# Attention in nine tiles of 512 columns per round where there were twelve of mixed width, and the second transpose of the first expert stage one slot sooner

## The reference

```python
# causal attention: 16 heads of 64, all in float32
s = einsum('bhid,bhjd->bhij', q * scale, k)
gm = max(s, axis=-1)                       # over all keys, the masked ones too
p = where(causal_mask, 0.0, exp(s - gm))
out = einsum('bhij,bhjd->bhid', p, v) / (sum(p, -1) + EPS)
...
# experts: 32 of 128 x 128, the two best of each token
w_masked = zeros_like(rw).at[arange(T)[:, None], idx].set(vals)
acc = acc + x_flat * w_e[:, None] @ W_e    # for each expert
```

## Time and profile before

| | |
|---|---|
| median of 3 runs | 1938.06 us (1935.25 to 1942.48) |
| the profiled execution | 1936.94 us, span 1935.2 us |
| PE, matmul busy | 1785.5 us (92%) |
| DVE | 1447.8 us (75%) |
| POOL | 1309.6 us (68%) |
| ACT | 1007.9 us (52%) |
| granted TensorE clock, mean | 0.958 |

### The profile page before, as it was taken

How to read it: one execution, slowest core, us unless ns; L and a number is a source line. 1 busy time by engine, 2 the same in 40 slices (tenths; PEclk the granted TensorE clock), 3 DMA queues, 4 the chain that set the end, 5 groups by cost and what they waited for, 6 DMA issues and landing times. The chain is left out here.

```text
span 1935.2 us, 32851 instructions
## 1 busy us (share of the span) xinstructions
PE 1785.5 (92%) x11830; PEld 1301.3 (67%) x11830; DVE 1447.8 (75%) x2497; ACT 1007.9 (52%) x2066; POOL 1309.6 (68%) x1327
## 2 busy tenths in 40 slices
PE   6999999999999999999999999959998478849998
PEld 4767667676767776767766767648776355538886
DVE  6777777777777777777777777559888166778998
ACT  3444444444445454444444444447887555437776
POOL 1777667667776676676666766839888245617998
PEclk9999999999999999999999999979999588969999
DMA  3000000000000000000000000000000000000000
GB/s 89 2 1 1 1 1 1 1 1 1 1 2 1 1 1 1 1 1 1 1 1 2 1 1 1 23 22 1 1 1 1 7 1 1 1 0 7 12 12 17
DMA packets 15089, 10.89 MB, mean 6 GB/s; under 512 B 433, under 2 KB 14546, under 8 KB 14930
## 3 DMA queue, kind: packets, MB, share of 16 engines
q1 hardware_dynamic: 14930, 8.80, 1.6%
HBM read 6.70 MB, written 2.10 MB: 5 GB/s over the span
## 5 line engine op out<-in xcount | busy, mean ns | idle before, releaser
L1222 DVE TENSOR_REDUCE attn_neg<-attn_shared 128x2 f32<-128x1024 f32 x512 | 614.7, 1223 | 272.7 <-PE attn_shared L1355 268.8
L1105 ACT ACTIVATE attn_prob<-attn_shared 128x1024 f32<-128x1024 f32 (+3 forms) x384 | 311.2, 813 | 451.6 <-PE attn_shared L1383 350.9
L1017 POOL TENSOR_TENSOR attn_row_sum<-attn_row_sum,attn_prob 128x1024 f32<-128x1024 f32 (+3 forms) x256 | 417.2, 1630 | 129.7 <-ACT attn_prob L1105 110.0
L497 ACT ACTIVATE experts_weighed<-experts_y,kept_gate 128x128 f32<-128x128 f32 x1024 | 279.0, 404 | 68.2 <-PE experts_y L724 53.6
L1012 POOL TENSOR_TENSOR attn_row_sum<-attn_prob 128x1024 f32<-128x1024 f32 x64 | 135.4, 2116 | 217.7 <-ACT attn_prob L1105 215.2
L580 DVE SCALAR_TENSOR_TENSOR experts_acc<-experts_y,kept_gate,experts_acc 128x128 f32<-128x128 f32 x960 | 262.4, 340 | 20.9 <-PE experts_y L724 18.9
L1351 PE MATMUL attn_shared<-attn_qk_hi 64*128 64x512 f32 x1024 | 226.5, 425 | 11.4 <-DVE attn_qk_lo L1235 2.4
L1241 DVE RECIPROCAL attn_den<-attn_den 128x256 f32<-128x256 f32 x128 | 214.7, 1719 | 12.1 <-ACT attn_den L1129 12.1
L1355 PE MATMUL attn_shared<-attn_qk_hi,attn_qk_lo 64*128 64x512 f32 x1024 | 211.3, 392 | 0.0
L1353 PE MATMUL attn_shared<-attn_qk_lo,attn_qk_hi 64*128 64x512 f32 x1024 | 210.2, 390 | 0.0
L722 PE MATMUL experts_y<-kept_w_hi,kept_xT_hi 128*128 128x512 f32 x512 | 205.9, 402 | 0.1
(11 more groups left out here) (227 smaller groups left out, 3265.2 us busy)
## 6 DMA issues: line engine op xcount, KB each, us to landing
kept_x<-in_L_attn_a_x_dram SPq DMA_DIRECT2D x4, 512.0 KB, 9.3
out_dram<-kept_x SPq DMA_DIRECT2D x8, 256.0 KB, 2.3
attn_prob<-in_L_attn_a_Wkv_dram SPq DMA_DIRECT2D x2, 512.0 KB, 6.9
kept_half_raw<-_ffn_expert_weights_dram SPq DMA_DIRECT2D x2, 512.0 KB, 4.5
last_other_half<-_ffn_expert_weights_dram SPq DMA_DIRECT2D x2, 512.0 KB, 4.6
attn_prob<-in_L_attn_a_Wq_dram SPq DMA_DIRECT2D x1, 512.0 KB, 5.1
attn_wo<-in_L_attn_a_Wo_dram SPq DMA_DIRECT2D x1, 512.0 KB, 5.4
attn_bo<-in_L_attn_a_bo_dram SPq DMA_DIRECT2D x1, 64.0 KB, 5.5
```

The source lines that it names most:

```text
L497: ins = act.activation(weighed[n][:, e, :], y[fill(pair, quad, odd) % RING][:, e * D:(e + 1) * D], ACT.Copy, scale=k.gate[:, c, quad * PER ...
L1017: pool.tensor_tensor(row_sum[n][:, :, at:], row_sum[n][:, :, at:], src[:, :, at:], ALU.add).then_inc(add_ok, 1)
L1105: act.activation(prob[n % RING][:, :, at:], buffer((p, i))[:, :, at:], ACT.Exp).then_inc(exp_ok, 1)
L1222: dve.tensor_reduce(neg[p % 2][:, :, b, half], buffer((p, b, half))[:, :, :], AX.X, ALU.max, negate=True).then_inc(max_ok, 1)
```

## The change

The twelve parts of a round are kept, in another order, and grouped into nine tiles. A tile is two banks of PSUM, one per head, of 512 columns. The narrow parts share a tile by twos: 384 with 128 columns, 256 with 256, and 384 with 128. The exponential is one instruction of 512 columns per head for each tile. Masks, additions and products still go by part. The order of the row stages is now a string for each of the two, and the nine tiles of a round just fill the ring of nine. In the expert stage the second transpose comes 8 slots after the base in place of 9, and `high` and `low` stand first behind the weighing and the gated sums.

```diff
-    STATS, VARIANCE, ROOT, SCALE, NORMAL, TURN = (-7, 0), 1, 2, 3, ((4, 4), (5, 6)), (6, 9)
+    STATS, VARIANCE, ROOT, SCALE, NORMAL, TURN = (-7, 0), 1, 2, 3, ((4, 4), (5, 6)), (6, 8)
...
                     weigh(pair, turn)
+                    for half in range(2):
+                        if turn_at(slot, half) is not None:
+                            high(turn_at(slot, half), half)
...
                     quad_sums(pair, turn)
+                    for half in range(2):
+                        if turn_at(slot, half) is not None:
+                            low(turn_at(slot, half), half)
                     if turn == 2 and pair:
                         merge(pair - 1)
...
-    ST_UNITS = [(1, j) for j in (0, 1, 2, 5, 6, 7, 3, 4)] + [(0, j) for j in range(4)]
+    PARTS = [(1, j) for j in (0, 1, 2, 5, 7, 3, 4, 6)] + [(0, j) for j in range(4)]
+    TILES = [[(1, 0)], [(1, 1)], [(1, 2)], [(1, 5), (1, 7)], [(1, 3)], [(1, 4)], [(1, 6), (0, 2)], [(0, 0)], [(0, 1), (0, 3)]]
+    FIRST_TILES, FIRST_PARTS = 5, 6
+    HALF_TILES = 7
-    STAGE = "stststststssst"
-    UNITS = len(ST_UNITS)
+    STAGES = ("stststststsss", "stsstsstssts")
+    UNITS = len(PARTS)
...
+    def place_of(part):
+
+        at = 0 if part != TILES[tile_of(part)][0] else columns(part)
+        return slice(at, at + HALF - columns(part))
...
-            def exponential(p, i):
-                n = UNITS * p + i
-                at = columns(i)
-                old_p, old_i = divmod(n - RING, UNITS)
+            def exponential(p, t):
+                n = len(TILES) * p + t
+                old_p, old_t = divmod(n - RING, len(TILES))
                 act.wait_ge(shift_ok, n + 1)
                 if n >= RING:
-                    act.wait_ge(pv_ok, n - RING + 1)
-                    act.wait_ge(add_ok, ADDS * old_p + ADDED[old_i])
+                    last = max(PARTS.index(part) for part in TILES[old_t])
+                    act.wait_ge(pv_ok, UNITS * old_p + last + 1)
+                    act.wait_ge(add_ok, ADDS * old_p + ADDED[last])
...
-                act.activation(prob[n % RING][:, :, at:], buffer((p, i))[:, :, at:], ACT.Exp).then_inc(exp_ok, 1)
+                act.activation(prob[n % RING][:, :, :], buffer((p, t))[:, :, :], ACT.Exp).then_inc(exp_ok, 1)
...
+            def shifted(p, t):
+
                 hi, lo, neg_row = qk_hi[p % 2], qk_lo[p % 2], neg_rows
+                shared_free((p, t))
+                for part in TILES[t]:
+                    half, j = part
+                    if part in ((1, 0), (0, 2)):
+                        pe.wait_ge(rows_ok, 2 * p + 2 - half)
+                    keys = slice(j * P, (j + 1) * P)
+                    at = slice(half * HALF + columns(part), (half + 1) * HALF)
+                    out = buffer((p, t))[:, :, place_of(part)]
...
```

More of the change, by code:

```diff
@@ L816, in out_group, with columns, tile_of, tile_count @@
         return g if r % 2 and 0 <= g < ROUNDS // 2 else None
-    def columns(i):
-        half, j = ST_UNITS[i]
+    def columns(part):
+        half, j = part
         return max(0, (j - 4 * half) * P)
+    def place_of(part):
+        at = 0 if part != TILES[tile_of(part)][0] else columns(part)
+        return slice(at, at + HALF - columns(part))
+    def tile_of(part):
+        return next(n for n, tile in enumerate(TILES) if part in tile)
+    def tile_count(p, i):
+        return len(TILES) * p + tile_of(PARTS[i]) + 1
     def is_diagonal(i):
-        half, j = ST_UNITS[i]
+        half, j = PARTS[i]
         return j >= 4 * half
@@ L914, in halves_done, with slot @@
             return max(0, 2 * n - 1)
+        def slot(p, part):
+            return prob[(len(TILES) * p + tile_of(part)) % RING]
         def buffer(u):
@@ L989, in mask @@
             def mask(p, i):
-                at = columns(i)
-                diagonal = prob[(UNITS * p + i) % RING][:, :, at:at + P]
-                pool.wait_ge(exp_ok, UNITS * p + i + 1)
+                at = place_of(PARTS[i]).start
+                diagonal = slot(p, PARTS[i])[:, :, at:at + P]
+                pool.wait_ge(exp_ok, tile_count(p, i))
                 pool.tensor_tensor(diagonal, diagonal, below[:, :].unsqueeze(1).to_broadcast([P, 2, P]),
@@ L998, in add @@
             def add(p, i):
-                half, j = ST_UNITS[i]
+                half, j = PARTS[i]
                 n = 1 - half
-                at = columns(i)
-                src = prob[(UNITS * p + i) % RING]
+                at = columns(PARTS[i])
+                src = slot(p, PARTS[i])[:, :, place_of(PARTS[i])]
                 if i in (0, 8):
@@ L1048, in _ @@
                         normal(r - 1, 0)
-                    for p, i in turned_units(r, t):
+                    for p, i in parts(r, t):
                         if is_diagonal(i):
@@ L1364, in turned @@
                 ins.then_inc(turned_ok, 1)
-            def shifted(p, i):
-                half, j = ST_UNITS[i]
+            def shifted(p, t):
                 hi, lo, neg_row = qk_hi[p % 2], qk_lo[p % 2], neg_rows
[L1370 to L1383, removed]
+                shared_free((p, t))
+                for part in TILES[t]:
+                    half, j = part
+                    if part in ((1, 0), (0, 2)):
[3 more added lines that the diff above has]
+                    out = buffer((p, t))[:, :, place_of(part)]
+                    for h in range(2):
+                        pe.matmul(out[:, h, :], hi[head(h), 1, keys], hi[head(h), 0, at], start=True, stop=False)
+                    for h in range(2):
+                        pe.matmul(out[:, h, :], hi[head(h), 1, keys], lo[head(h), 0, at], start=False, stop=False)
+                    for h in range(2):
+                        pe.matmul(out[:, h, :], lo[head(h), 1, keys], hi[head(h), 0, at], start=False, stop=False)
+                    for h in range(2):
+                        ins = pe.matmul(out[:, h, :], pick[head(h), :], neg_row[head(h), at], start=False, stop=True)
@@ L1384, in shifted @@
                 ins.then_inc(shift_ok, 1)
             def product(p, i):
-                half, j = ST_UNITS[i]
-                g, first = p // 2, columns(i)
+                part = PARTS[i]
+                half, j = part
+                g, first = p // 2, columns(part)
                 if i == 0:
@@ L1396, in product @@
                 else:
-                    pe.wait_ge(exp_ok, UNITS * p + i + 1)
+                    pe.wait_ge(exp_ok, tile_count(p, i))
                 for h in range(2):
                     cols = slice((2 * (p % 2) + h) * DH, (2 * (p % 2) + h + 1) * DH)
-                    ins = pe.matmul(pv[head(h), first:], v[g % 2][:, j, cols], prob[(UNITS * p + i) % RING][:, h, first:],
+                    ins = pe.matmul(pv[head(h), first:], v[g % 2][:, j, cols], slot(p, part)[:, h, place_of(part)],
                                     start=(j == 0), stop=(i in (7, 11)))
```

33 lines of the change are left out of this document (14 added, 19 removed).

## The result

The changed kernel takes 1913.87 us, the median of 4 runs (1912.57 to 1914.20), against 1936.92 for the kernel before in the same comparison. A fourth run of the kernel before, 1935.79 us, moved its median from 1938.06. The ratio is 0.9875, with a 95% interval of 0.9854 to 0.9896: faster, by 23 us between the medians and 24 by the ratio, 1.2% and clear of the noise. In a second comparison it was 0.9878 (0.9865 to 0.9892).

What follows compares the result with a forecast made beforehand. PE was taken to bound attention, losing time to PSUM waits, and to stall at routing in the expert stage. 18.9 + 7.0 - 0.5 = 25.4 us off the 1938.06 median gave 1912.7 us, range 1896 to 1930.

Steps and rivals of the forecast that it cites:

- PE bounds attention, and its loss is holes in the row stages: Attention: PE sets the pace; holes are waits for PSUM, and unit order can give at most 1.12 us a round.
- The first row stage, 0.07 gained: First row stage of a round: no unit held, margin only 0.1 us, 10.65 us for 10.72.
- The second row stage, 10.24 laid out: Second row stage: one hold of 0.4 us plus 0.08 restart, 10.24 us for 10.78, 0.54 gained.
- Behind the second stage: After the second row stage: the next waits for DVE, which also ends 0.57 us earlier, so PE's gain is kept.
- Sum of attention, 18.9 less 0.5: Attention: 0.61 us in each of 31 rounds, 18.9 us, less 0.5 once for GpSimd's additions in the last round.
- Fewer exponentials count for nothing: Attention, ScalarE: nine exponentials for twelve save 0.5 us a round, worth nothing as ACT has 19 us idle.
- The experts, 7.0: Expert stage: an earlier transpose removes two routing stalls, 8.4 us, partly taken back; 7.0 taken, bounds 8.4 and 2.
- The rival without holds: Attention: DVE's lead carries over the "s s t" pattern, so no holds; 43 us gained in all, 1895 us; chance 0.12.
- the holes only move: Row stages: thin margins become waits that eat the attention gain, only the experts' gain stays, 1931 us; chance 0.09.
- The routing does not stall: Expert stage; the rival judged said the routing stalls as before, by the clock or another transpose, 1920 us; chance 0.12.
- The lockstep rival: Second row stage runs in lockstep with DVE, takes 12.54 us, and the kernel is slower at 1983 us; chance 0.03.
- The rule of the Trainium skill: PE in row stages: short rests while cycling PSUM banks swing the clock between two levels, so more to gain.

Runs made afterwards that it cites:

- e7: Changed kernel with the second row stage ordered s t s t s t s t s s s s (s scores, t turned): 1907.1 us, ratio 0.9833.
- e9: Changed kernel with the second-stage order of e7 and one of VectorE's two second-stage reciprocals moved behind the low parts: 1906.3 us, ratio 0.9840.
- e10: Changed kernel with only one of VectorE's two second-stage reciprocals moved behind the low parts: 1914.6 us, ratio 0.9879.
- e1: Kernel before with the expert part alone: second transpose 8 slots after the base, high and low moved up in their queues: 1930.2 us, ratio 0.9957.
- e4: Kernel before with only high and low moved to the front of their queues, transposes left in slots 28, 44 and 60: 1935.7 us, ratio 0.9984.
- e8: Changed kernel with two exponentials for each packed tile, one per part, tiles and order as changed: 1914.9 us, ratio 0.9874.
- e3: Kernel before with only the second transpose 8 slots after the base, high and low still last in their queues: 1927.4 us, ratio 0.9944.
- e5: Changed kernel in the same order, but each part in its own tile, twelve tiles and a ring of ten: 1983.2 us, ratio 1.0228.

## Why the prediction was right, point by point

It said 1912.7 us in a range of 1896 to 1930, and 1913.87 was measured.

- **PE bounds attention, and its loss is holes in the row stages**: right. PE's work stayed the same, the holes shrank, and the time of a round followed.
- **The first row stage, 0.07 gained**: none was. Two terms were misread and cancel. The packed tile of 384 and 128 was costed at 1.22 and takes 1.10 (615.00 to 616.10), because 0.12 of the 0.52 read for the 128 part belongs to what follows a stage, not to the part. Now the last score unit bears it, with 0.83 (619.23 to 620.06) for the 0.70 put down. What is missing is at the last unit, where the margin of 0.1 us was indeed too thin: the unit ahead of it takes 0.77, a hold with its restart.
- **The second row stage, 10.24 laid out**: 10.28. The hold at the fifth score unit was put at 0.4 and a restart of 0.08, and it is 0.35 and 0.07. The rest of the agreement is partly luck: the packed tile takes 1.09 for 1.22 (637.14 to 638.23), and the last unit 0.87 for 0.70 (638.23 to 639.10).
- **Behind the second stage**: the forecast that nothing is taken back was right, with a rest of 7.36 us for 7.38. The reason given was wrong. That step said that the next row stage waits for the low parts of VectorE. It does not (e7, e9, e10), and so the layout of e7 could be passed over.
- **Sum of attention, 18.9 less 0.5**: 16.3 less 1.3. A round gained 0.52 for 0.61. The 0.5 for the last round was right: GpSimd makes the product wait there, and it starts its first addition without a rest, where it had rested 1.13 us, because it comes out of the round before with more work left. The other 0.8 is the clock in the last output product, 0.61 for 0.70, of which the sum had nothing. What sets that clock was not tested, but it is not the change alone: with attention as before the product takes 5.1 us in e1 and 5.9 in e4.
- **Fewer exponentials count for nothing**: right (e8).
- **The experts, 7.0**: 7.1 in the profiles (7.3 from first to last fill) and 7.5 alone (e1). The price of a stall, a wait and a fall of the clock behind it, held: the same fills, counted across the two stalls, come 4.1 and 4.3 us sooner, together the 8.4 of the sum. What was taken back held in size only. The 1.2 us put down for ScalarE are not in the trace, where the longest delay of a fill between the transposes of slots 27 and 43 and their routings is 0.24 us. Instead 0.4 us are lost at the start of the stage, where the clock is low for longer (the 31st fill comes 11.82 us after the first for 11.44), and 0.7 in slots 50 to 58, which no run explains. But the place in the queues, on which the prediction counted too, added nothing (e3).
- **Not foreseen**: 2.2 us of the profiled gain come from the two lengths of the linear stage and are no part of the change. So the closeness of the forecast is partly luck: without them the profiled gain is 22.2 us for the 25.4 of the sum. That the forecast started from a median of 1938.06, and not 1936.92, brought it another 1.1 us nearer to the time measured.
- **The rivals.** The rival without holds did not come, as two maxima in a row did cost PE 0.35 us. That the holes only move did not come either: where units of 512 columns alternate, they follow one another after 0.92 and 0.70. The routing does not stall, 0.29 us behind the last fill, with `low` 0.06 us ahead of it. The lockstep rival did not come; what does run slower than before is the unpacked order of e5.
- **The rule of the Trainium skill** (TensorE: Matmul & The Clock Gate, "A second HAM failure mode: psum-queue depth-cycling") was set against the row and did not hold here. The granted clock is 1.00 through the rounds of the kernel before, with holes of 0.3 us in each row stage, and removing holes gave their own length and no more. The page tells it of another kernel, in bf16, and gives no length of the rests.

Of the versions tried, e7 beats the kernel before by 31 us and the changed one by 7. It differs from the change in one string. e9 is as fast and has more edits.

## What to carry to other kernels

When an engine reads as busy all the time, read the starts of its units and compare each kind of unit with its own shortest distance: the sum of the excess is what an order can give. A narrow tile in a ring of PSUM buffers takes a whole buffer, so try to pack narrow parts by twos (here 1914 us for 1983), and try more than one order of the units, since the layout by hand found the large holes here and not the best order (e7, 7 us less). Before a chain of waits is taken to bound a stage, look in the code at which of its steps the first unit waits for.

## What the runs showed of the hardware

- After a rest of PE of 2.52 or 2.54 us the matmuls of 512 columns came every 0.43 us for a while. After rests of 1.96 and 1.95 us in one run (e4) they came every 0.23 us the first time and every 0.43 the second. So a rest of 1.96 us costs about 2 us or about 3.6, an estimate that adds 1.6 for the lower clock.
- The linear stage, in which PE rests many times, has one of two lengths, 205.3 to 205.5 or 207.6 to 208.3 us, and both occur for the same kernel. A difference of 2 us in such a stage between two single profiles says nothing of a change.
- The same output product of 32 matmuls took 5.30 us at a granted clock of 0.70 and 6.08 at 0.61, behind waits of 6.16 and 6.15 us; with the same attention code it took 5.1 in e1 and 5.9 in e4.
- A score unit ahead of a matmul of another kind (L1424 or L1385) takes 0.83 or 0.87 us, medians of the changed kernel, in place of 0.70. Why was not tested.
